# A GpSimd copy behind each send of a job's results in a decoder layer

## The reference, cut to what matters

```
x = x + self_attention(layernorm(x))
x = x + cross_attention(layernorm(x), ctx, mask)
h = layernorm(x);  xn = layernorm(h) * gamma + beta
probs = softmax(clip(xn @ router_w.T));  top 2 experts of each token
for eid in range(8):
    gu = (xn * gate[:, eid]) @ gate_up_w[eid].T        # 128 -> 2 x 256
    out += (silu(gu[:, :256]) * gu[:, 256:]) @ down_w[eid].T
x = x + (h + out)
```

## Time and profile before

| | |
|---|---|
| runs | 262.64 us median (262.19 to 265.65) |
| the profiled execution | span 285.5 us, the only time that is shown of it; one core, mean granted TensorE clock 0.944 |
| busy | TensorE 232.3 us (81%), VectorE 197.1 (69%), ScalarE 145.4 (51%), GpSimd 127.6 (45%) |
| chain that ended last | TensorE 60%, issue 13%, DMA 8%, VectorE 6%, GpSimd 4% |
| sends (L2044) | 39, 978 ns mean, from 193.0 to 273.6 us |

### The profile page before, as it was taken

The page is one execution under the profiler, slowest core; times in us unless marked ns, Lnnn a source line. Parts: engine busy times, 40 slices in busy tenths (PEclk is TensorE's granted clock), DMA queues, the critical chain, the costliest instruction groups (busy, mean ns, idle before and its releaser), DMA issues.

```text
span 285.5 us, 9442 instructions
## 1 busy us (share of the span) xinstructions
PE 232.3 (81%) x3293; PEld 191.6 (67%) x3296; DVE 197.1 (69%) x874; ACT 145.4 (51%) x335; POOL 127.6 (45%) x184
## 2 busy tenths in 40 slices
PE   6799999999989999999997785765497679797900
PEld 2776788778868777877775553655496679797900
DVE  2567677988988888878787876784648447364333
ACT  2457677767757766766576444370132235243400
POOL 1122333234356555643743643367454655445430
PEclk9999999999999999999999999599689999799765
DMA  7996996000000000000000003682428748664256
GB/s 232 246 395 245 406 407 246 2 6 0 13 23 13 9 21 13 21 15 12 29 5 19 21 22 106 200 220 94 112 72 251 223 148 253 188 201 127 93 176 201
DMA packets 24526, 36.31 MB, mean 127 GB/s; under 512 B 3726, under 2 KB 14225, under 8 KB 24224
## 3 DMA queue, kind: packets, MB, share of 16 engines
q1 hardware_dynamic: 20272, 29.98, 32.8%
q0 software_dynamic: 2272, 4.27, 4.3%
q10 hardware_dynamic: 1936, 1.46, 1.7%
HBM read 21.26 MB, written 14.89 MB: 127 GB/s over the span
## 4 chain that ended last, share of the span: by engine, by line
PE 60%; issue 13%; DMA 8%; DVE 6%; POOL 4%; ACT 3%; another core or an unknown queue 2%; SPq 2%; DVEq 0%; POOLq 0%; ACTq 0%
PE six L505 47%; PE few_bank L505 5%; DMA g_sb<-slots 3%; PE six L605 2%; DMA bcst_f<-in_bconsts 2%; PE six L840 2%; POOL rstd L1945 2%; PE turn_bank L505 2%; DMA y_all<-results 1%; DMA results<-y_sb,meta 1%; POOL slots L2002 1%; ACT jsilu L1087 1%; PE turn_bank L516 1%; ACT oT_sb L977 1%
## 5 line engine op out<-in xcount | busy, mean ns | idle before, releaser
L1945 POOL TENSOR_TENSOR rstd<-var,cst 128x1 f32<-128x1 f32 (+1 forms) x32 | 25.3, 791 | 85.2 <-DVE var L1294 59.5
L2044 POOL DMA_INDIRECT results<-y_sb,meta x39 | 38.1, 978 | 35.8 <-ACT y_sb L977 13.3
L505 PE MATMUL six<-gT_sb,gu_sb 128*128 128x128 f32 x312 | 46.9, 300 | 0.0
L505 PEld LDWEIGHTS six<-gT_sb,gu_sb 128*128 128x128 f32 x312 | 43.3, 215 | 0.3
L2002 POOL DMA_INDIRECT slots<-pay,slot_i x32 | 32.8, 1026 | 9.5 <-issue 7.9
L1087 ACT ACTIVATE jsilu<-six 128x256 f32<-128x256 f32 x39 | 14.9, 385 | 36.7 <-PE six L505 23.9
L1676 DVE TENSOR_TENSOR hidT<-jsilu,six 128x256 f32<-128x256 f32 x39 | 16.2, 417 | 24.9 <-ACT jsilu L1087 15.9
L505 PE MATMUL six<-downT_sb,hidT 128*128 x156 | 25.8, 294 | 1.0 <-DVE y_sb L1702 0.8
L840 PE MATMUL six<-cst,xw_sb 128*128 128x128 f32 x39 | 12.4, 317 | 15.9 <-ACT gT_sb L977 9.8
L505 PEld LDWEIGHTS six<-downT_sb,hidT 128*128 128x128 f32 x156 | 22.2, 207 | 1.5 <-issue 1.4
L1023 ACT ACTIVATE etanh<-six,xscale 128x1024 f32<-128x1024 f32 x16 | 17.8, 1114 | 8.2 <-PE six L505 8.2
(11 more groups left out here) (160 smaller groups left out, 562.0 us busy)
## 6 DMA issues: line engine op xcount, KB each, us to landing
gu_sb<-in_guT SPq DMA_DIRECT2D x39, 256.0 KB
slots<-empty_sb SPq DMA_DIRECT2D x16, 528.0 KB, 5.9
g_sb<-slots SPq DMA_DIRECT2D x39, 66.0 KB
ctxT_all<-in_ctxT SPq DMA_DIRECT2D x1, 1024.0 KB, 9.8
downT_sb<-in_downT SPq DMA_DIRECT2D x1, 1024.0 KB, 8.7
y_all<-results SPq DMA_DIRECT2D x4, 256.0 KB, 3.9
x_all<-in_x SPq DMA_DIRECT2D x2, 320.0 KB, 5.4
results<-y_sb,meta POOLq DMA_INDIRECT x39
```

What stands on the lines that cost most here:

```text
L505: return pe.matmul(o, lhsT=l, rhs=r, start=start, stop=stop, **kw)
L1945: nc.gpsimd.tensor_tensor(dst, src, half[:, 0:dst.shape[1]], ALU.pow).then_inc(semaphore, 1)
L2044: nc.gpsimd.indirect_dma_start(results, bass.IndirectOffsetOnAxis(meta[j % (2 * RING)][:, 0:1].bitcast(I32), 0), y_sb[k][:, :], None, boun ...
```

## The change

`send` gets a copy of 256 float32 numbers a partition on GpSimd, from the input tile `x_all` (loaded at the start and never written again) to a new buffer `pause_sb` that nobody reads. It stands behind the indirect DMA of each of the 39 jobs. Its completion raises the new semaphore `paused`, and from job 1 on GpSimd waits, before the copy, until the copy of the job before has finished.

```diff
+        pause_sb = sb("pause_sb", [P, 2, D])
...
+        paused = sem("paused")
...
                     y_sb[k][:, :], None, bounds_check=TOPK * TOK - 1,
                     oob_is_err=False).then_inc(y_out[k], 16)
+                if j > 0:
+                    pool.wait_ge(paused, j)
+                nc.gpsimd.tensor_copy(pause_sb[:, :, :], x_all[:, 0:2, :]).then_inc(paused, 1)
```

## The result

The changed kernel took 270.14 us in the median of four runs (269.60 to 271.45), the kernel before 262.77 us: ratio 1.028, 95% interval 1.023 to 1.034, +7.4 us. Beside other kernels, on one chip and in more rounds, it was 1.026 (1.021 to 1.032).

A forecast was written before the change was run, and what follows sets the result against it. Limits per job were put at GpSimd 1.27 us, TensorE 1.47 and the profiled stage 1.94 (1.78 in runs, over the new step 1.60). 262.64 + 0.3 for a last bunch + 0.26 for send 36 = 263.2 us; range 261.2 to 268.4.

The forecast's parts named there:

- The bound: Job stage, sends 1 to 35: limits per job are GpSimd 1.27 us, TensorE 1.47, the stage as profiled 1.94.
- rival 1: Sends 13 to 38: GpSimd becomes the pacemaker, costing 4.4 to 10.2 us; chance 0.12 over 2%, 0.18 for 1.5 to 5 us.
- The step: Distance between sends on GpSimd with a copy behind each: taken as 1.60 us, bounds 1.27 and 1.66.
- In the profiled execution: Last sends of the 285.5 us trace: send 35 moves by 0.01 us, counted 0; +0.26 if send 36 is waited for.
- The early sends: Sends 0 to 12: copy 0 delays six scatters by 0.3 to 0.4 us, covered by SyncE's wait for VectorE's table.
- The ring: Buffers `y_sb` come free six jobs on, 11.7 us; a send with landing takes under 4, so ScalarE's copy doesn't wait.
- The shared way into SBUF: VectorE's `weigh_rows` steps and the GpSimd copy both read SBUF: 0 in the sum, 4.1 us at the upper end.
- The meeting the other way round: GpSimd's copy held up by VectorE's SBUF reads: up to 0.35 us on GpSimd's step, making it 1.95.
- Rival 2: Job stage: the copies break up bunches of sends and remove ScalarE's idle holds, 6 us faster, 256.6 us; chance 0.08.
- Rival 3: Between sends: the copy hides in GpSimd's idle 0.30 us and costs nothing, 262.6 us; chance 0.12.

The follow-up runs named there:

- second profile: The kernel before, unchanged, profiled a second time: span 261.5 us at a run of 263.43 us.
- early copies: Against the kernel before, the copy added behind the sends of jobs 0 to 12 alone: ratio 1.003 (0.999 to 1.007), median 264.13 us.
- late copies: Against the kernel before, the copy added behind the sends of jobs 13 to 38 alone: ratio 1.016 (1.008 to 1.023), median 266.41 us.
- memset of 376: Against the changed kernel, a GpSimd memset of 376 numbers in place of the copy: ratio to the kernel before 1.025, median 269.96 us.

## Why the prediction was wrong, point by point

**The bound.** The prediction had all three numbers: GpSimd's step 1.27 us, TensorE's 1.47, the stage as profiled 1.94. The third failed. In the second profile, whose span fits the runs, it is 1.41, not the 1.78 that I took in proportion. Nor did "it can't be under TensorE's 1.47" hold: the sends of the stage begin behind and catch up, so they follow each other faster than the results do. The stage gave up 65.86 - 47.95 = 17.9 us of the 24.0 that lay between the two profiles (285.5 and 261.5). I had named just that, 16 of 22.9 us, as the argument against rival 1, since the stage is only 23% of the span. This is the step that failed: the gaps of a long execution were spread over the kernel in proportion, and so the stage was credited with slack over 1.60 that isn't there. The rows had shown gaps in just this place, TensorE idle for 10 of 66 us, so the stage without them had to be priced with more weight.

**The step.** 1.60 us was taken, 1.57 worked out, 1.56 measured; the copy took 0.41 where 0.42 was taken. Right.

**In the profiled execution.** "Send 35 moves by 0.01" may hold for that execution, which no run can show, and says nothing of the runs: its idle 1.80 us in front of send 34 is 0.48 us in the second profile, with 0.55 in front of send 35, at steps of 1.47.

**The early sends.** The scatters' delay of 0.3 us was put at 0, covered by the wait for the table. That looked at SyncE alone. Send 1 stands behind the same six scatters and is 4.4 us late in the second profile; in the first profile the result of job 1 came at 203, after the scatters were done, and so the backlog wasn't visible. By itself the early part is still cheap, as the early copies showed. Together with the late ones it isn't, since what GpSimd is behind is then no longer worked off: early and late copies alone lost 0.7 and 4.2 us by their ratios, both together 7.0.

**The ring.** "ScalarE's copy doesn't wait" was wrong: it waited 6.3 us in 8 times. Six jobs, put at 11.7 us (6 x 1.94 is 11.6), are 6 x 1.56 = 9.4, and late in the stage a send starts 5.2 us after its result.

**The shared way into SBUF.** The sum had 0, and the change's loss needs nothing for it, as the memset of 376 shows within 1.8 us; the range's 4.1 us wasn't needed. The meeting the other way round, "up to 0.35 on GpSimd's step", was seen at 0.14 (0.55 for 0.41), in the copies behind every other send.

**The forecast and the rivals.** Rival 1 happened, with its mechanism and its mark (steps alike at 1.56 us, save where a sum stands between). Its place, the sends from 13 on, is right in part: of the 6.9 us that the profiles differ by from send 1 to send 35, 2.8 come before send 13 and 4.1 behind it. It had 0.12 for a loss of over 2%, which is what came, and 0.18 for less. Its price of 4.4 us was too low, because it took 1.47 us for the step before, where 1.41 was measured. The estimate above gives +6.4 us for send 35; the profiles show 54.86 - 47.95 = 6.9 us, and the runs +7.4 us. Rival 2, the bunches, is out: in the second profile TensorE has no idle time from 220 to 240 us that could be won back. Rival 3 is out by the step.

## What to carry to other kernels

Before adding work to an engine, compare its step with the steps of the others in the densest stretch of the stage, not with the average: here added time was free up to a step of some 1.37 us, by the estimate from the result times, 0.1 us below TensorE's 1.47, and cost its whole length above 1.47. When the profiled execution is much longer than the runs, its slack is not to be trusted, nor to be shrunk in proportion; ask for each gap whether it would be there in a run of the median's length, and price the change for the stage without gaps as a case of its own weight. An engine that is behind at the start of a stage needs slack in every later step to recover, so a queue's backlog belongs into the sum.

## What was not expected of the hardware

A GpSimd copy that reads SBUF and a VectorE instruction with two SBUF inputs can lock in step for more than ten jobs, the copy undisturbed at 0.41 to 0.42 us, the other at 0.53 to 0.54 in place of 0.35. Begun 0.04 us after the VectorE instruction, such a copy took 0.55 us itself. A memset on GpSimd that took about as long, 0.43 us, left the VectorE instruction at a mean of 0.357. The Trainium skill, "SBUF — State Buffer", Who interferes with whom, states that such an instruction contends with GpSimd reads and not with pure writes, and that the order of issue decides which of the two waits. In both points the traces agree. In size they don't: a wait for all of the copy, as the prediction took from that section, would have made 0.38 + 0.35 = 0.73 us of the instruction at 236.04, and it took 0.53.

One profile of an unchanged kernel had a span of 285.5 us and another 261.5 us, at granted clocks of 0.944 and 0.951; in the job stage they were 0.91 and 1.00. What held the first one up wasn't found.
